# A decoder layer on one core: a new order of every engine's list, six of eight score turns in pairs, one identity product for the positions

## The reference

```python
x = x + self_attention(layernorm(x))         # 16 heads of 8, rotary positions, causal, biases
x = x + cross_attention(layernorm(x), ctx)   # 16 heads of 8, 77 keys
n = layernorm(x)
p = softmax(n @ router_w)                    # 8 classes
shared = (n @ sup * silu(n @ sgate)) @ sdown # 128 -> 512 -> 128
e = argmax(p)                                # experts 0 to 6 exist, class 7 has none
routed = (n @ up[e] * silu(n @ gate[e])) @ down[e]
return x + 2 * p[e] * routed + shared
```

## Time and profile before

| | |
|---|---|
| median of 3 runs | 1129.05 us (1126.96 to 1132.03) |
| profiled execution, span from first to last instruction | 1100.5 us |
| own time of the profiled execution around the span | not given apart; the median is 28.5 us over the span |
| TensorE busy over the span | 1043.7 us (95%), 16352 products |
| TensorE weight loads | 890.1 us (81%), beside the products |
| VectorE / ScalarE / GpSimd busy | 858.9 (78%) / 732.1 (67%) / 629.3 us (57%) |
| granted TensorE clock, mean | 0.986 of full |
| chain that ended last | TensorE 88%, issue 2%, GpSimd 2%, all others 1% or less |

### The profile page before, as it was taken

One profiled execution on the slowest core, in us unless ns is written; L12 is line 12 of the kernel. 1 busy time (PEld: TensorE's weight loads), 2 busy tenths in 40 slices (PEclk: granted clock), 3 DMA queues, 4 the chain that ended last, 5 costly groups with the idle time before them and its releaser, 6 DMA issues.

```text
span 1100.5 us, 50361 instructions
## 1 busy us (share of the span) xinstructions
PE 1043.7 (95%) x16352; PEld 890.1 (81%) x16353; DVE 858.9 (78%) x2853; ACT 732.1 (67%) x1557; POOL 629.3 (57%) x1488
## 2 busy tenths in 40 slices
PE   2789999999999999999999999999999879999995
PEld 2567888888888888888888888888887879999995
DVE  3358888888888888888888888888886447777774
ACT  0367777777777777777777777777775235555552
POOL 0345666666666666666666666666664314444443
PEclk9799999999999999999999999999999989999998
DMA  5132111011011000110001110111100032222220
GB/s 102 37 101 73 57 30 37 27 25 25 25 34 26 25 25 25 33 27 25 25 25 33 27 25 25 25 33 28 28 23 26 27 91 63 74 70 69 70 68 5
DMA packets 66668, 44.50 MB, mean 40 GB/s; under 512 B 24135, under 2 KB 61451, under 8 KB 66592
## 3 DMA queue, kind: packets, MB, share of 16 engines
q1 hardware_dynamic: 55424, 30.35, 10.7%
q0 software_dynamic: 5312, 12.18, 3.3%
q10 hardware_dynamic: 5856, 0.99, 0.7%
HBM read 23.96 MB, written 18.29 MB: 38 GB/s over the span
## 4 chain that ended last, share of the span: by engine, by line
PE 88%; issue 2%; POOL 2%; DVE 1%; ACT 1%; DMA 0%; SPq 0%; POOLq 0%; DVEq 0%; ACTq 0%
PE pv L1190 11%; PE scores L1077 6%; PE scores L1374 6%; PE scores L1232 6%; PE scores L1379 6%; PE ro L1391 6%; PE scores L1239 5%; PE ro L1247 5%; PE st L1302 5%; PE pj L1213 4%; PE scores L1111 4%; PE ro L1207 3%; PE ro L1199 3%; PE scores L1103 3%; PE ro L1287 3%
## 5 line engine op out<-in xcount | busy, mean ns | idle before, releaser
L992 ACT ACTIVATE arena<-scores 128x1024 f32<-128x1024 f32 (+1 forms) x256 | 261.9, 1024 | 55.3 <-PE scores L1111 49.1
L669 DVE TENSOR_REDUCE arena<-scores 128x8 f16<-128x1024 f32 (+1 forms) x256 | 254.5, 994 | 25.3 <-PE scores L1085 14.8
L914 ACT ACTIVATE arena<-st 128x128 f16<-128x128 f16 (+2 forms) x256 | 155.1, 606 | 23.8 <-PE st L1324 14.6
L1190 PE MATMUL pv<-arena 128*32 128x128 f32 (+1 forms) x4096 | 139.8, 278 | 0.3 <-ACT arena L992 0.3
L449 POOL TENSOR_TENSOR arena<-arena,neg_half 128x1 f32<-128x1 f32 x192 | 107.5, 560 | 28.7 <-POOL arena L440 10.5
L1190 PEld LDWEIGHTS pv<-arena 128*32 128x32 f32 (+1 forms) x4096 | 105.0, 110 | 15.1 <-ACT arena L992 0.8
L676 DVE STREAM_TRANSPOSE arena<-pv 128x256 f32<-128x256 f32 x128 | 57.0, 445 | 47.8 <-PE pv L1190 47.7
L914 ACT ACTIVATE arena<-arena 128x512 f16<-128x512 f32 (+2 forms) x192 | 92.5, 482 | 2.5 <-DVE arena L710 1.4
L550 POOL DMA_INDIRECT out_dram<-x_tile x70 | 69.5, 992 | 39.0 <-POOL carried L549 26.6
L1077 PEld LDWEIGHTS scores<-causal 32*128 32x128 bf16 x2048 | 47.3, 92 | 54.2 <-issue 52.7
L440 POOL TENSOR_TENSOR arena<-arena,eps 128x1 f32<-128x1 f32 x192 | 36.6, 190 | 81.6 <-DVE arena L651 81.6
(11 more groups left out here) (175 smaller groups left out, 2804.6 us busy)
## 6 DMA issues: line engine op xcount, KB each, us to landing
x_tile<-xs SPq DMA_DIRECT2D x70, 129.0 KB, 2.1
arena<-arena SPq DMA_DIRECT2D x512, 4.0 KB
arena<-in_x_dram SPq DMA_DIRECT2D x64, 64.0 KB, 2.2
out_dram<-pay SPq DMA_DIRECT2D x64, 64.0 KB, 2.2
arena<-in_ctx_dram SPq DMA_DIRECT2D x64, 38.5 KB
w_gate<-in_L_ffn_gate_w_dram SPq DMA_DIRECT2D x7, 256.0 KB, 2.7
w_up<-in_L_ffn_up_w_dram SPq DMA_DIRECT2D x7, 256.0 KB, 3.0
w_down<-in_L_ffn_down_w_dram SPq DMA_DIRECT2D x7, 256.0 KB, 4.0
```

The lines of the kernel that those rows point to most:

```text
L669: v.tensor_reduce(nmax[:, n, :].rearrange("p (m r s) -> p r m s", r=2, s=SLOT)[:, u, :, 0:HG], pair(s)[:, :, 0:HG * keys].rearrange("p m ( ...
L914: return a.activation(to, of, ACT.Copy)
L992: a.activation(e32[0:rows, 2 * n + u, :], scores[0:rows, 1024 * s:1024 * (s + 1)], ACT.Exp).then_inc(sexp_done[n][u], 1)
L1190: last = t.matmul(pv[SLOT * j:SLOT * (j + 1), 0:2 * P].rearrange("p (c a y) -> p a c y", a=2, y=SLOT)[:, a], vals[0:rows, p, at0:at0 + SLO ...
```

## The change

All five lists get a new order and new lags. `LAG` becomes 13, so 16 steps are unrolled ahead and the last 13 behind. The shared products use half 0 of `scores` (before: half 1). Three pairs take the place of one. `positions` has one product by the identity for both results. In TensorE's list:

```diff
-two_turns(i, p, self_exp, 6, 0, 1, (...), self_exp, 6, 1, 0, (...))
-at(i, p, 5, self_for_max, 1, 0, ...)
-at(i, p, 5, self_for_max, 0, 1, ...)
-at(i, p, 9, cross_for_exp, 1, 0, ...)
-at(i, p, 9, cross_for_exp, 0, 1, ...)
+two_turns(i, p, self_max, 7, 1, 0, (((sh_hid, -5),), ((sexp_done[1][1], -3),), ((sexp_done[0][1], -1),), ((smax_done[0][1], 0),),),
+          self_exp, 8, 0, 1, (((smax_done[1][1], -1),), ((smax_done[1][0], -1),), ((sexp_done[1][0], -2),), ((smax_done[0][0], 1),), ((sexp_done[0][0], 0),),))
+two_turns(i, p, self_exp, 8, 1, 0, (((smax_done[0][1], 2),), ((sh_hid, -4),), ((sexp_done[1][1], -2),), ((sexp_done[0][1], 0),),),
+          self_max, 7, 0, 1, (((sexp_done[0][0], 0),), ((smax_done[1][1], -2),), ((smax_done[1][0], -2),), ((sexp_done[1][0], -3),), ((smax_done[0][0], 0),),))
+two_turns(i, p, cross_exp, 10, 1, 0, (((sexp_done[0][1], 3),), ((smax_done[0][1], 4),), ((sh_hid, -2),), ((sexp_done[1][1], 0),),),
+          cross_exp, 10, 0, 1, (((smax_done[0][0], 4),), ((sexp_done[0][0], 3),), ((smax_done[1][1], 1),), ((smax_done[1][0], 1),), ((sexp_done[1][0], 0),),))
```

(The tuples in the removed lines are cut; they stand in the listing above.) The positions:

```diff
-                for n, before_in in enumerate((earlier, ones16)):
-                    cols = ro[:, 2 * P + n * E:2 * P + (n + 1) * E]
-                    t.matmul(cols, before_in[:, :], hot16[:, p, :], start=True, stop=False)
-                    last = t.matmul(cols, id32[:, :], run_base[:, :], start=False, stop=True)
+                cols = ro[:, 2 * P:2 * P + 2 * E].rearrange("p (n e) -> p n e", n=2)
+                t.matmul(cols, id32[:, :], run_base[:, :].unsqueeze(1).to_broadcast([P, 2, E]), start=True, stop=False,
+                         skip_group_check=True)
+                t.matmul(cols[:, 0], earlier[:, :], hot16[:, p, :], start=False, stop=False, skip_group_check=True)
+                last = t.matmul(cols[:, 1], ones16[:, :], hot16[:, p, :], start=False, stop=True, skip_group_check=True)
```

More of the change, by code:

```diff
@@ L21 @@
 EPS = 1e-5
-LAG = 15
+LAG = 13
 LATE = 56
@@ L522, in step @@
             def step(i, p):
-                at(i, p, 11, k2_low)
-                at(i, p, 8, rope_add)
-                at(i, p, 8, rope_bias_in)
-                at(i, p, 10, scaled, 0)
-                at(i, p, 8, qk_low)
-                at(i, p, 15, scatter)
-                at(i, p, 13, ln_rstd_of, 2)
-                at(i, p, 7, ln_rstd_of, 0)
-                at(i, p, 13, ln3_shift_of)
-                at(i, p, 10, ln_rstd_of, 1)
-                at(i, p, 12, scaled, 1)
-                at(i, p, 14, token_of)
-                at(i, p, 7, add_out_bias, 0)
-                at(i, p, 11, add_out_bias, 1)
-                at(i, p, 10, q2_low)
+                at(i, p, 4, scaled, 0)
+                at(i, p, 1, ln_rstd_of, 0)
+                at(i, p, 2, qk_low)
+                at(i, p, 0, add_out_bias, 0)
+                at(i, p, 7, ln_rstd_of, 2)
+                at(i, p, 7, token_of)
+                at(i, p, 4, ln_rstd_of, 1)
+                at(i, p, 7, ln3_shift_of)
+                at(i, p, 4, k2_low)
+                at(i, p, 8, scatter)
+                at(i, p, 4, q2_low)
+                at(i, p, 5, add_out_bias, 1)
+                at(i, p, 6, scaled, 1)
+                at(i, p, 1, rope_add)
+                at(i, p, 1, rope_bias_in)
             run(pool, step)
@@ new lines, in step @@
+                at(i, p, 8, hidden_of, 0)
+                at(i, p, 8, hot_pos_of)
+                at(i, p, 8, run_of)
+                at(i, p, 5, row_max, 1, 1, 1)
+                at(i, p, 4, k2_bias)
+                at(i, p, 8, put_of)
+                at(i, p, 0, ln_stats_of, 0)
+                at(i, p, 4, ln_mean_var, 1)
+                at(i, p, 8, gate_of)
+                at(i, p, 8, add_shared)
+                at(i, p, 2, row_max, 0, 1, 0)
+                at(i, p, 4, q2_bias)
+                at(i, p, 6, turned, 1)
@@ L1123, in self_for_max, with self_for_exp @@
                     self_max_round(s, u, p, g)
+            def self_for_exp(b, p, u, s, now, *before):
+                wait(pe, max_rows[0][p], 32 * b + 64 - 32 * p)
+                turn(pe, b, now, *before)
+                for h in range(4):
+                    mask_round(s, u, 1, h)
+                for g in range(HG):
+                    self_exp_round(s, u, p, g)
             def cross_for_max(b, p, u, s, now, *before):
```

165 lines of the change are left out of this document (73 added, 92 removed).

## The result

The changed kernel took 1145.98 us (median of 4 runs, 1143.74 to 1158.88) beside 1129.68 (1126.96 to 1132.03) for the kernel before: ratio 1.0163, 95% interval 1.013 to 1.0197. It is 16 us slower, clear of the noise; 1090 was forecast. Its profiled execution has a span of 1141.9 us, 1.8 less than its own time.

What follows compares the result with a forecast made beforehand. TensorE was taken as the bound at 12.52 us a step; new pieces 11.40 plus waits 0.1, 0.33, 0.1 gave 11.95. Steps -37, lead-in +5, drain -9, last base +1.7: 1129.05 - 39 = 1090 us, range 1062 to 1112.

Steps and rivals of the forecast that it cites:

- Point 2: Ahead of the cross exponent pair: TensorE waits 0.33 us (0.2 to 0.8) for row maxima by DMA, 4.48 less 4.15.
- point 1: Ahead of the second self pair: TensorE waits about 0.1 us (0 to 0.25) for VectorE to free both score-bank halves.
- The sign that the prediction named for it: Mid loop: TensorE idle before the cross exponent pair, ended by the DMA of the row maxima; TensorE 95 to 96% busy.
- Elsewhere I find margins of 0.1 to 0.9 us and charge nothing: All other hand-overs in the new step: enough slack everywhere, so no wait was added to the step.
- Rival C: GpSimd's queue, with scatter and q2_low in a row, slows the loop: 1153 us at 1.5 us late; chance 0.03.
- So a step now costs what TensorE's pieces add up to: Kernel before, mid loop: TensorE busy all 300 us, so its pieces set the step of 12.52 us.
- the saving of the cross pair: Cross exponent turns on TensorE: 0.41 and 0.25 become one pair of 0.30, saving 0.36 us (0 to 0.41).
- 28.5 more, which lies around the span and stays: Whole kernel: median 1129.05 exceeds the profiled span 1100.5 by 28.5 us, taken as constant time outside the span.
- Points 1 and 3: The second named here: ahead of the next x transpose, TensorE waits 0.1 us (0 to 0.5) for ScalarE's queue.
- Fill and drain: Loop's ends: lead-in +5 us (0 to +7); drain -9 (-12 to -3), two last cross-pair steps 9.5 each.
- Rival D: Pairs of different turns don't overlap over the strips: step about 12.95 us, time 1153; chance 0.02.
- Rival A: The forecast waits don't come up: step 11.45 us, time 1060, between 1055 and 1075; chance 0.17.

Runs made afterwards that it cites:

- e13: Changed kernel with the indirect scatter replaced by a plain DMA to fixed blocks, placing by class left out; quick level: 1104.79 us, ratio 1.0028.
- e3: Changed kernel with the turns of each pair issued one after the other; quick level: 1115.09 us, ratio 1.0113.
- e16: Changed kernel unaltered, run again and traced at the quick level: 1112.4 us in its one run, beside 1101.44 for the kernel before.
- e9: Kernel before, unaltered, run again for a trace at the slow level: 1130.08 us.
- e4: Kernel before with only the new positions (one identity product over both halves); quick level: 1100.30 us, ratio 0.999.
- e2: Kernel before with its scatter moved six pieces later in GpSimd's step, behind token_of; quick level: 1372.95 us, ratio 1.2452.
- e12: Kernel before with the new positions, the up product sooner, a cross score turn and add_cross later; slow level: 1176.66 us, ratio 1.0409.
- e17: Changed kernel with the path of the cross row maxima started sooner on TensorE, VectorE and ScalarE; slow level: 1191.03 us, ratio 1.0551.
- e8: Changed kernel with the scatter one piece earlier on GpSimd, ahead of k2_low; slow level: 1139.51 us, ratio 1.0087.
- e11: Changed kernel with the turns of each pair issued one after the other, at the slow level: 1143.71 us, ratio 1.0129.
- e1: Changed kernel with the scatter moved to the end of GpSimd's step; quick level: 1130.32 us, ratio 1.0258.
- e6: Changed kernel with turns issued one after the other and the scatter last on GpSimd; slow level: 1153.19 us, ratio 1.0224.
- e5: Changed kernel unaltered, run again at the slow level: 1147.30 us, ratio 1.0161.
- e10: Changed kernel unaltered, run once more at the slow level in a later series: 1148.06 us, ratio 1.0184.

## Why the prediction was wrong, step by step

1. **Point 2, the row maxima by DMA, was mis-sized: 0.33 (0.2 to 0.8) forecast, 0.95 measured at the quick level.** This is the step that failed in size. The way took 4.90 us (4.89 from 521.27 to 526.16) where 4.48 was taken from the earlier trace rows, the end of the loop; and the pieces between take 3.95, not 4.15, in part since point 1's wait didn't come. The sign that the prediction named for it did: idle time ahead of the cross exponent pair, ended by the DMA (0.78). The wait is there with and without the scatter (e13: 0.66 idle), and single turns are simply absorbed by it (e3). At the slow level the way is hidden: the cross pair comes 5.3 us behind the transpose, later than the maxima need.
2. **"Elsewhere I find margins of 0.1 to 0.9 us and charge nothing" failed.** Every other step TensorE waits for its own sequencer ahead of `ctxT_of`, behind the edge of the loop (0.33 idle, e16; 0.23 a step on average). In the kernel before the steps alternate by 0.05 only. `turned_back` costs 0.16. With 0.95 from point 2, TensorE's own 11.34 becomes 12.68, the measured step.
3. **The slow level's own term was not foreseen.** The new order puts the end of the cross values under the scatter, and the second self pair takes 1.04 us more. Rival C looked at the scatter for its length on GpSimd's list, not for what it does to TensorE. In a regular step the changed kernel is nevertheless behind by as much at either level (0.17 quick, 0.14 slow): the hole takes the place of the wait for the maxima. Without the falls of the clock, two of 3 us in its trace and none in e9's, the slow level would show no more loss than the quick one.
4. **"So a step now costs what TensorE's pieces add up to" failed for the kernel before.** Busy 300 of 300 meant that TensorE was never seen idle, not that it was the longest chain. Shown by e4: 0.30 us less on TensorE, nothing in the step (12.52 for 12.53). The cross turn priced at 0.41 held 0.16 of a wait; the saving of the cross pair was 0.15, not 0.36. This is not what made the miss: the pieces of the changed step add up to 11.34 (forecast 11.40; cross pair 0.35 for 0.30 and not the 0.48 or 0.66 also considered, positions 0.32 for 0.37). That so close a sum came out is in part luck, since other pieces got cheaper (shared down 0.89, before 1.03; up 0.89, before 0.97).
5. **"28.5 more, which lies around the span and stays" was wrong.** Around the span are 2 us. The 28 lay in the steps of another level, where TensorE's completions come late behind the scatter. I should have asked why this trace ended 28 us sooner than the runs.
6. **Points 1 and 3** cost nothing to be seen: no wait ahead of the second self pair, none of ScalarE ahead of the x transpose.
7. **Fill and drain**: -9 was forecast for the drain, -1.6 and -3.8 came. At the quick level the two last steps with a cross pair took 10.48 and 12.79 us (cross values to cross values), not 9.5 each; what held them was not looked for. The lead-in was in its bounds.
8. **Rival D** (no overlap) was wrong, as forecast. Rival A (no waits) fell with item 1; its sum gives 1061, not 1060. No rival was built on the waits being larger on the way through DMA, or on the kernel before already having a second chain as long as TensorE's list.

## What to carry to other kernels

What an engine's pieces add up to is the least that a new order can cost; the waits decide the rest. A way through another engine and a DMA that is hidden now becomes a bound when work is taken from between its ends, so measure it in the middle of the loop and compare it with what is left between. An engine that is busy all the time may be level with a ring through another engine: compare two distances of the same piece, or take one small piece off the engine and see if the step gets shorter; here this costs one edit. Compare a trace's own time with the median before adding any difference as a constant. And each list position moved moves what its bank or buffer waits for: e2, e12 and e17 each lost more by such a wait (45 to 270 us) than was to be gained.

## What the runs showed of the hardware

**An indirect scatter on GpSimd delays completions of TensorE's score turns and values, and no other engine's.** I took from the traces, between 200 and 800 us, each instruction that counts a semaphore up, and the time from its end to the count, apart for those that end within the 1.07 us of a scatter. The median in us:

| | level | elsewhere | TensorE within a scatter | VectorE within |
|---|---|---|---|---|
| before | quick | 0.014 | 0.019 | 0.011 |
| before (e9) | slow | 0.014 | 0.614 | 0.011 |
| changed (e16) | quick | 0.014 | 0.471 | 0.011 |
| changed | slow | 0.014 | 1.078 | 0.011 |
| scatter 0.3 sooner (e8) | slow | 0.014 | 1.059 | 0.011 |
| turns single (e3; e11) | quick; slow | 0.014 | 0.193; 0.867 | 0.011 |
| scatter last (e1) | quick | 0.014 | 0.014 | 0.011 |

At the slow level it follows the scatter from place to place (e6: values on time, the cross turn 0.56 late), and at the quick level no product is late with a plain DMA in the same place (e13, against 0.47 to 0.51 behind the second self pair in e16). So the scatter is shown as its condition; the two levels rest on different runs. The medians mix pieces: the float32 products of the gate, the shared down, the output projection and q2 that end within a scatter are on time in every trace (0.014, the gate at the slow level too, e6), so e1's row shows a place where nothing sensitive stood. Late are score turns, values, and small products right behind them (a transpose in e6 by 0.33). Why the size depends on the level and on the piece is open. ScalarE's completions within a scatter (changed kernel) were at 0.010. The Trainium skill ("SBUF — State Buffer", SBUF: two separate sides) says that TensorE and ScalarE never wait on another engine for memory, only VectorE and GpSimd share a port. These runs don't tell whether memory is what TensorE waits for, but VectorE, which by that page can be the one to suffer, did not.

**Losing 0.7 us can cost 3 more.** The clock fell in two of the changed kernel's steps with the hole between 400 and 700 us; at the quick level, with the same list of instructions, the granted clock was 1.00 over the whole of that stretch. In the four slow traces with this standstill (changed, e5, e10, e8) there are ten falls between 200 and 800 us, and each begins 0.69 to 0.79 us behind the end of one. There is a standstill in each step, some 45 in each trace; the others were followed by none.
